# Attention loop of a gated cross-attention kernel: output product behind the keys, its split in the next step, joins behind the first maximum, layer-norm work spread over the steps

## What is computed

```
def _L0_xattn_ref(q, k, v, Wq, Wk, Wv, Wo, bo, mask):
    qh = split_heads(q @ Wq)            # 16 heads of 64
    kh = split_heads(k @ Wk)
    vh = split_heads(v @ Wv)
    dots = einsum('bhid,bhjd->bhij', qh, kh) * SCALE     # masked and causal
    attn = softmax(dots)
    out = einsum('bhij,bhjd->bhid', attn, vh)
    return out @ Wo + bo
x = x + tanh(g_xattn[0]) * _L0_xattn_ref(_layernorm(x), ctx_1024, ctx_1024, ...)
x = x + tanh(g_ffn[0]) * _L0_ffn_ref(_layernorm(x), w_gate, w_up, w_down)
```

## Time and profile before

| | us |
|---|---|
| median of 3 runs | 1814.12 (1812.88 to 1816.78) |
| the profiled execution | 1819.5, its span 1817.7 |
| PE busy | 1588.7 (87%) |
| DVE busy | 1492.1 (82%) |
| ACT busy | 1259.1 (69%) |
| POOL busy | 778.9 (43%) |
| attention part | from the start to about 1245 |

### The profile page before, as it was taken

How to read it: one execution, slowest core, us unless ns; L and a number is a source line. 1 busy time by engine, 2 the same in 40 slices (tenths; PEclk the granted TensorE clock), 3 DMA queues, 4 the chain that set the end, 5 groups by cost and what they waited for, 6 DMA issues and landing times. The chain is left out here.

```text
span 1817.7 us, 38253 instructions
## 1 busy us (share of the span) xinstructions
PE 1588.7 (87%) x12684; PEld 1285.3 (71%) x12684; DVE 1492.1 (82%) x2624; ACT 1259.1 (69%) x3238; POOL 778.9 (43%) x622
## 2 busy tenths in 40 slices
PE   7798888988889889898898988887998999895998
PEld 5676776767767677676676766666776777674887
DVE  6787878878788788787887878876888899898997
ACT  5576776766767666676666666665765899896665
POOL 3445545555455454454545545451000666560000
PEclk9899999999999999999999999989999899897999
DMA  5434434434344343344433533243996788474664
GB/s 168 110 83 106 88 88 92 102 86 92 82 92 105 88 98 82 81 107 92 92 82 81 117 82 92 54 87 113 341 327 224 264 279 302 149 289 174 196 208 150
DMA packets 351460, 252.22 MB, mean 139 GB/s; under 512 B 287792, under 2 KB 325808, under 8 KB 348464
## 3 DMA queue, kind: packets, MB, share of 16 engines
q1 hardware_dynamic: 351408, 251.58, 49.1%
HBM read 105.25 MB, written 76.02 MB: 100 GB/s over the span
## 5 line engine op out<-in xcount | busy, mean ns | idle before, releaser
L423 POOL TENSOR_TENSOR prob<-prob,rsums 128x512 f32<-128x512 f32 x256 | 265.5, 1040 | 560.1 <-DVE rsums L625 560.1
L474 ACT ACTIVATE prob<-masked,neg_max 128x128 f32<-128x128 f32 x1024 | 396.5, 389 | 154.5 <-DVE neg_max L637 153.2
L428 POOL TENSOR_TENSOR prob_parts<-prob,prob_parts 128x512 f16<-128x512 f32 x254 | 295.1, 1180 | 3.2 <-ACT prob_parts L482 1.5
L882 PE MATMUL pv<-probT,v_sb 128*64 128x128 f32 x2048 | 154.7, 283 | 112.3 <-DVE probT L617 89.6
L882 PEld LDWEIGHTS pv<-probT,v_sb 128*64 128x64 f32 x2048 | 111.2, 137 | 170.4 <-DVE probT L617 109.5
L482 ACT ACTIVATE prob_parts<-prob 128x512 f16<-128x512 f32 x254 | 160.1, 630 | 68.0 <-POOL prob L423 66.3
L674 DVE TENSOR_TENSOR o_lo<-pv,o_hi 128x512 fp32r<-128x512 f32 x125 | 86.4, 691 | 132.5 <-ACT o_hi L527 132.2
L474 ACT ACTIVATION_READ_ACCUMULATOR prob<-masked,neg_max 128x1 f32 x1024 | 192.6, 188 | 0.0
L637 DVE TENSOR_REDUCE neg_max<-masked 128x4 f32<-128x512 f32 x254 | 174.3, 686 | 8.8
L617 DVE TENSOR_TENSOR probT<-turn 128x512 f32<-128x512 f16 x254 | 172.4, 719 | 3.4 <-DVE mask_add L647 3.4
L635 DVE TENSOR_TENSOR masked<-score,mask_add 128x512 f32<-128x512 f32 x254 | 173.1, 682 | 1.6
(11 more groups left out here) (252 smaller groups left out, 4404.0 us busy)
## 6 DMA issues: line engine op xcount, KB each, us to landing
gate<-gate_d SPq DMA_DIRECT2D x30, 768.0 KB, 4.3
n_x<-n_x_d SPq DMA_DIRECT2D x25, 512.0 KB, 5.0
gate_d<-stage SPq DMA_DIRECT2D x8, 1536.0 KB, 5.5
n_u_d<-w_raw SPq DMA_DIRECT2D x16, 768.0 KB, 4.0
stage<-n_u_d SPq DMA_DIRECT2D x16, 768.0 KB, 5.9
gate_d<-gate SPq DMA_DIRECT2D x7, 1536.0 KB, 5.5
x_in<-in_x SPq DMA_DIRECT2D x16, 512.0 KB, 4.2
ctx_in<-in_ctx SPq DMA_DIRECT2D x16, 512.0 KB, 5.1
```

The lines of the kernel that those rows point to most:

```text
L423: gp.tensor_tensor(prob[:, h], prob[:, h], rsums[:, h, :].rearrange("p (b o) -> p b o", o=1).broadcast_to([P, NB, P]), ALU.mult).then_inc( ...
L428: gp.tensor_tensor(prob_parts[:, h, 1], prob[:, h].rearrange("p b k -> p (b k)"), prob_parts[:, h, 0], ALU.subtract).then_inc(prob_low, 1)
L474: nc.scalar.activation(prob[:, h, b, :], masked[:, h, b, :], ACT.Exp, bias=neg_max[:, h, b:b + 1], accum_out=psums[:, h, b:b + 1]).then_in ...
L882: last = nc.tensor.matmul(pv[h * HD:(h + 1) * HD, b, :], v_sb[:, b, c * P + h * HD:c * P + (h + 1) * HD], probT[:, h, b, :], start=True, s ...
```

## The change

On PE, the key projection comes right behind the query projection and ahead of the output product. In c = 7 the first transpose stands between keys and output product, and the other three behind the output product, behind the place of the values, and behind `times_v`.

On DVE, the second half's maximum comes behind the joins; `o_lo` is no longer made in the step of its `times_v` but in the next step, behind the first maximum; the scaling of the sums leaves DVE; the extras are moved between the two reciprocals, some of them cut in two; the rest of an extra comes behind the second reciprocal, where the value copies now are too.

On POOL, a small product `scaled` takes the place of the scaling, with a wait of POOL on itself; the bias is added in c = 6 instead of c = 5. On ACT, `kT` stands between the exponentials of the halves in every step, and in c = 7 the four `high` copies are spread.

```diff
@@ the order of jobs over the two banks @@
-        jobs += [(c, "q", 0)]
-        if c == NC - 1:
-            jobs += [(c, "t", n) for n in range(KC)]
-        jobs += [(c, "k", 0)]
+        jobs += [(c, "q", 0), (c, "k", 0)]
         jobs += [(c, "v", n) for n in V_AT[c]]
-    jobs += [(NC - 1, "t", n) for n in range(KC, 2 * KC)]
+    jobs += [(NC - 1, "t", n) for n in range(2 * KC)]
@@ POOL @@
             def normalise_prob(u, h):
                 gp.wait_ge(recip_done, 2 * u + h + 1)
-                gp.tensor_tensor(prob[:, h], prob[:, h], rsums[:, h, :]...
+                gp.tensor_tensor(scaled[:, h], rsums[:, h], pscale[:], ALU.mult).then_inc(sum_scaled, 1)
+                gp.wait_ge(sum_scaled, 2 * u + h + 1)
+                gp.tensor_tensor(prob[:, h], prob[:, h], scaled[:, h, :]...
...
+                if c == 6 and new:
                     gp.wait_ge(xres_loaded, 16 * (g + 1))
                     gp.tensor_tensor(xres[:], xres[:], bo_g[:]...
@@ ACT @@
                 if soft:
                     exps(u - 1, 0)
-                if new and k_first:
+                if nxt:
+                    high(g, *ts[0])
+                if new:
                     copy_k(g, c, u)
                 if nxt:
-                    high(g, *ts[KC])
+                    high(g, *ts[1])
                 if soft:
                     exps(u - 1, 1)
-                if new and not k_first:
-                    copy_k(g, c, u)
@@ DVE @@
-                nc.vector.tensor_scalar(psums[:, h, :], psums[:, h, :], 1.0 / PSCALE, None, ALU.mult).then_inc(sum_scaled, 1)
-                dve.wait_ge(sum_scaled, 2 * u + h + 1)
                 nc.vector.reciprocal(rsums[:, h, :], psums[:, h, :]).then_inc(recip_done, 1)
...
                 if soft:
+                    maxima(u - 1, 0)
+                if oldest:
+                    attended_low(u - 4)
                 if old:
                     for h in range(2):
                         join_prob(u - 3, h, (c + 1) % 2, NC // 2 * g + (c - 1) // 2)
                 if soft:
+                    maxima(u - 1, 1)
                     reciprocals(u - 1, 0)
+                if c == 0:
+                    make_mask(g)
+                if c == 1 and more:
+                    layernorm_stats(g + 1)
+                if c == 2 and more:
+                    layernorm_moments(g + 1)
+                if c == 3 and after_first:
+                    residual(g)
+                if c == 4 and after_first:
+                    second_stats(g - 1)
+                if c == 5 and after_first:
+                    second_norm(g - 1, 0, NB // 2)
+                if c == 6 and after_first and more:
+                    second_max(g - 1)
                 if nxt:
+                    for n in range(2):
+                        low(g, *ts[n], 2 * KC * (g + 1) + n)
                 if soft:
                     reciprocals(u - 1, 1)
+                if c < 3:
+                    values(g, c)
+                if c == 4 and after_first:
+                    second_moments(g - 1)
+                if c == 5 and after_first:
+                    second_norm(g - 1, NB // 2, NB)
+                if c == 6 and more:
+                    normalise(g + 1)
                 if nxt:
+                    for n in range(2, 4):
+                        low(g, *ts[n], 2 * KC * (g + 1) + n)
@@ PE @@
                     weights_left(g, c, jobs_of(c, "q")[0][0], 0)
+                if new:
+                    weights_left(g, c, jobs_of(c, "k")[0][0], 1)
                 if nxt:
                     transpose_in(g, *ts[0])
                 if oldest:
...
                     out_product(u - 4, (c - 4) % NC)
                 if nxt:
                     transpose_in(g, *ts[1])
-                if new:
-                    weights_left(g, c, jobs_of(c, "k")[0][0], 1)
-                if nxt:
-                    transpose_in(g, *ts[2])
```

132 lines of the change are left out of this document (56 added, 76 removed).

## The result

The changed kernel takes **1751.17 us** (median of 4 runs, 1750.21 to 1754.21), against 1815.45 for the kernel before (4 runs, 1812.88 to 1817.66): a ratio of **0.965, 95% interval 0.963 to 0.967**. The forecast was 1695 in a range of 1655 to 1755. The direction is right, and the time lies just inside the range, but outside the forecast's own stretch of 1670 to 1725. The gain is 64 us where 119 were forecast, and the second rival had given 1754. The profiled execution has a span of 1748.4 us and 1750.2 with what lies around it, from 1819.5: 69.3 less.

The account below looks back on a forecast made before the run. Bound: the cycle DVE to ACT to DVE through `o_lo`. 46.3 + 21.0 = 67.3 us a pass from 75.04 saves 108 over 14 passes, plus 11 at the ends: profiled 1700, median 1695, range 1655 to 1755 (1670 to 1725: 0.6).

Parts of the forecast that it names:

- the second rival: DVE and POOL take turns: POOL's low part runs between joins; steps of 8.2 us, 1754 in all; chance 0.2.
- the cycle through `o_lo`: DVE to ACT to DVE bounds c = 2 to 6: 10.04 us around, against PE's 7.59 a step.
- Room behind the second reciprocal: On DVE, between a step's second reciprocal and the next first maximum: room for 1.1 us of extra work.
- 0.7 for both steps together: In c = 5 and 6, `xn2` and `x_in` meeting POOL's products and `xres` cost 0.7 us together.
- Joins ahead of the second maximum: On DVE: `times_v` waits of 1.25 and 2.19 us go; a join held about 0.6 fits the room.
- Keys ahead of the output product: On PE in each step: a wait of 0.66 us for `o_lo`, due with the old order, is avoided.
- Scaling on POOL: POOL's small product takes 0.225 us plus 0.05 for the wait; POOL's step, 4.9 of 7.59, is hidden.
- c = 7 and c = 0: 21.0: These two steps together: 18.9 us at the least, 22.8 at the most, 21.0 taken, from 22.29.
- The ends: 11: Groups 0 and 15, which also have start-up, weights and drain: 5.5 us saved each, 11 together (0 to 20).
- Fewer locks, short c = 7: Rival: c = 1 to 6 take 45.6 us, c = 7 and 0 18.9; 1652 in all; chance 0.1.
- The waits go elsewhere: Rival: waits of PE in c = 7 and 0 take back c = 1 to 6's gain; 1814; chance 0.04.
- Slower: Rival: a late DMA turn at the joins holds up the whole softmax; 51 us lost, 1865; chance 0.06.

Follow-up runs that it names:

- e3: The changed kernel with `o_lo` made in the step of its `times_v` again, behind the second reciprocal: 1818.43 us, ratio 1.002.
- e9: The changed kernel with `o_lo` back in the step of its `times_v` and the joins back behind both maxima: 1819.41 us, ratio 1.003.
- e10: The changed kernel with the layer norms' work of c = 1 to 6 uncut behind the second reciprocal again: 1855.29 us, ratio 1.022.
- e2: The changed kernel with the second layer norm's moments in c = 4 ahead of the second reciprocal instead of behind it: 1713.11 us, ratio 0.944.
- e5: The changed kernel with the joins back behind both maxima: 1692.07 us, ratio 0.933.
- e11: e8 with the scaling of the sums back on DVE instead of POOL: 1660.55 us, ratio 0.915.
- e8: The changed kernel in the planned order: joins behind both maxima, extras re-placed ahead of the first reciprocal or between the two, bias in c = 7: 1664.83 us.
- e7: The changed kernel with the scaling of the sums back on DVE and POOL's small product gone: 1797.12 us, ratio 0.990.
- e12: e8 with `o_lo` made in the step of its `times_v` again, behind the second reciprocal: 1760.36 us, ratio 0.969.
- e4: The changed kernel with the keys behind the output product again in c = 0 to 6: 1846.05 us, ratio 1.017.

## Why the prediction was half right

Its own working is for the profiled execution: 108 from the passes and 11 from the ends. Measured there: 61.35 and 8 (69.3 less 61.35). So 47 of the 50 us are missing from the passes, 3.4 in each: 2.3 in c = 1 to 6 (48.6 for 46.3) and 1.1 in c = 7 and c = 0 (22.06 for 21.0). The median lies 1 us above the profiled execution's time, where 5.4 below had been carried over from the run before.

- **What bounds the kernel: the cycle through `o_lo`.** Borne out, with a limit. Without the move the time is 1818 in this order and 1760 in the planned one: it is worth 67 and 96 us. But it doesn't bound c = 2 to 6 evenly. With the extras cut and placed as in the change, c = 1 to 4 run at 7.6 even with the cycle in place (e3, e9), so the 2.8 us gained in c = 2 and 3 don't need the moved `o_lo`.
- **Room behind the second reciprocal.** The prediction gave the extras "room for 1.1 us" at their lengths alone. The order is right: e10 shows 104 us for it. The lengths are not: the moments, 0.86 us alone, took 2.65, and the whole room was gone. The mis-sized term is "0.7 for both steps together" for locks in c = 5 and 6: c = 1 to 6 take 48.61 against 46.3, so they cost 3.0 (48.61 less 45.6). Nearly all of c = 5's 1.9 is the moments (e2).
- **Joins ahead of the second maximum: the step that failed.** I counted their waits of 1.25 and 2.19 as gained and put a held join at "about 0.6, often", "well inside the room". The waits of PE are gone, but they are nearly gone in e5 too, where the joins stand as before. The size of the holds in c = 1 to 4, 0 to 1.05, is about the 0.6 of the prediction, and the steps stay at 7.6. But they are not independent: each makes the next longer (in e5 all four are 1.28), and they use up the room that the moments and `xres` then need. In c = 4 a low part runs between them, and in c = 6 the pair was held for 3.21, since `xres` took its turn there, and what stands behind is no longer `times_v` alone but the softmax. This place costs 59 us. The prediction had the row from which it follows (two low parts taking 3.80 with a product between them) and used it for a rival only.
- **Keys ahead of the output product.** Right: 0.64 for 0.66 a step. The whole is larger, 95 us, since the key copy stands in ACT's queue ahead of the second half.
- **Scaling on POOL, "hidden".** The size was right (0.230 against 0.225). That it is worth 46 us in this kernel I had not seen; e11 shows that it isn't in another order.
- **c = 7 and c = 0: 21.0.** Measured 22.06. The prediction took one pass of the kernel before, 22.29 at a clock of 0.92, for what "now" is; the mean of the 14 passes was 21.47, so it had forecast 0.5 saved and 0.6 was lost. (The sum started from the mean pass of 75.04 all the same; the two windows of the earlier trace rows add up to 75.84.) The lower clock occurs in five passes of 14. The feared wait for the first transpose is 0.45; the longest is now the output product's 1.19 for `o_lo`. The 19.26 of e8 shows that the lower bound of 18.9 was near what can be had.
- **The ends: 11.** Measured 8. Group 0 hardly changed (81.6 to 81.2 us); the weights' work there still stands behind the second reciprocal.
- **The turn of the DMA, keys between the halves.** Right: no DVE wait on a DMA shows in 300 to 900 us.

**The rivals.** "DVE and POOL take turns" gave 1754, 3 us from the result, and its mechanism is real: in c = 4 a low part runs between two joins, and in c = 6 `xres` does. Its terms are near too: 49.2 for c = 1 to 6 and 22.0 for the rest, against 48.6 and 22.06. But the places are wrong. It had 8.2 us for each of the six steps; measured are 7.6 in c = 1 to 4, where the turns find room, and the excess is in c = 5 and 6, by the moments and `xres`, neither of which is in its cycle. That 49.2 comes so near is luck. The range held only because it had been drawn around this rival as well. "Fewer locks, short c = 7" (1652) is what e8 and e11 came near, 1665 and 1661, only after the order had been changed for it; as a number it lay 3 us under the range that was said to take it in. "The waits go elsewhere" came in small: c = 7 and c = 0 took back 0.6 of the 5.0 us. "Slower" did not come.

The parts don't add. Undone one at a time they cost 67 (`o_lo`), 95 (keys), 104 (extras) and 46 us (scaling) and give 59 (joins), and the sum of the change is 64. Each needs the others: a late half on DVE moves POOL's work onto DVE's next instruction, and a longer wait of PE can cost the clock on top (e7, e12).

Still open: 0.26 of e4's 0.90 a step is put down to ACT's queue by the row of the key copy alone; e10's 104 us are not split into gap and holds; why c = 7 loses 4.1 us in e12 is read from two waits and not tried; and the value of the weights' order in groups 0 and 15 wasn't tried.

## What to carry over

Where two engines exclude each other, a schedule made of undisturbed durations is wrong by the meetings: write down, for each instruction that can be held, what the other engine does at that moment, and put such instructions where the other has nothing to do. What is queued behind a held instruction sets its price: the same joins, held for 1.57 us behind the maxima and 3.21 ahead of one, cost 59 us more there. Fill an engine's idle time inside a cycle (here between two reciprocals) before shortening the work behind it.

## What the runs showed of the hardware

- **A waiting instruction gets the next turn, even between two that follow each other directly.** The bias addition began its record 0.6 us before the first join ended, and ran between two joins of one loop: 4.49 us instead of 1.28. In c = 4 a low part does the same, 2.33 instead of 1.28. The Trainium skill (SBUF — State Buffer, Who interferes with whom) calls the pair of ports that the two engines share an exclusive lock; of DVE's modes that take both ports it says that the engine which issues first holds the pair for the whole instruction and the other blocks fully. The holds here agree with it, those of the joins too.
- **A small instruction is held as long as a large one.** Operations on 4 columns, 0.16 us alone, took 1.01 to 1.19 beside POOL's product of 1.04 or low part of 1.15. It isn't only those with two inputs: `v_eps`, one tensor and two constants, took 1.03.
- **Some were never held.** Statistics took 1.37 and 1.41 for four parts, `amax_x` 1.18 and 1.19, also where POOL's product ran meanwhile (from 578.20, `amax_x` 577.76 to 578.95). The same section of the Trainium skill counts `tensor_reduce` on trn2 as never contending; the rows of `amax_x` agree. `masked` and `o_lo` have two inputs, one of them in PSUM, and weren't held either: of the kernel after's in 300 to 900 us none took over 0.70, with POOL at work beside 76 masks and 47 splits.
- **A wait can have a second price.** Behind the 3.84 us wait of e9, `times_v` took 1.97 for 1.09, and the granted clock of 754.1 to 769.9 was 0.82. Behind e7's wait of 2.93 it was 0.73 over 6.4 us. Behind the 1.61 us in c = 5 of the kernel after, the step's clock was 1.00 in all 14 passes. The length of a wait alone doesn't decide it: one pass of e7 keeps 1.00 behind the same 2.93, and the kernel before, with a wait of 2.05 or 2.06 in c = 7, has 1.00 in one pass (535.26) and 0.92 in another (609.54).
